# Cross attention in a decoder kernel: one product per head pair for values and key sums, and the division by query between two turns on TensorE

## What is computed

```python
q = (x @ Wq + bq).reshape(B, N, NUM_HEADS, HEAD_DIM)
k = (y @ Wk + bk).reshape(B, M, NUM_HEADS, HEAD_DIM)
v = (y @ Wv + bv).reshape(B, M, NUM_HEADS, HEAD_DIM)
scores = jnp.einsum('bnhd,bmhd->bhnm', q, k) * scale
attn = jax.nn.softmax(scores, axis=-1)
out = jnp.einsum('bhnm,bmhd->bnhd', attn, v).reshape(B, N, IMAGE_DIM)
h = jax.nn.relu(out @ W1 + b1)
return h @ W2 + b2
```

## Time and profile before

| | |
|---|---|
| Device time, three runs | 573.75, 574.8, 579.94 us; median 574.8 |
| Profiled execution, span from first to last instruction | 605.6 us |
| TensorE busy | 492.0 us (81%) |
| VectorE busy | 416.6 us (69%) |
| ScalarE busy | 297.0 us (49%) |
| POOL busy | 289.3 us (48%) |
| Granted TensorE clock, mean | 0.944 of full speed |

### The profile page before, as it was taken

The page is one execution under the profiler, slowest core; times in us unless marked ns, Lnnn a source line. Parts: engine busy times, 40 slices in busy tenths (PEclk is TensorE's granted clock), DMA queues, the critical chain, the costliest instruction groups (busy, mean ns, idle before and its releaser), DMA issues. The chain is left out here.

```text
span 605.6 us, 16577 instructions
## 1 busy us (share of the span) xinstructions
PE 492.0 (81%) x5675; PEld 367.1 (61%) x5675; DVE 416.6 (69%) x1308; ACT 297.0 (49%) x757; POOL 289.3 (48%) x540
## 2 busy tenths in 40 slices
PE   2979888888898888799999999998579887888820
PEld 1757666666666666467766766665357676676710
DVE  7568989998788878679989988875433323133337
ACT  2755556665655556246565655644153333223337
POOL 5454333333343331103577777768605665564630
PEclk9998999999999999689999999999699989797985
DMA  6643444555445553162333232311343323232149
GB/s 181 106 109 69 78 71 67 104 112 117 95 96 109 103 109 95 40 148 55 88 80 99 75 98 79 97 35 45 100 113 94 93 83 84 73 90 74 47 143 299
DMA packets 96002, 58.30 MB, mean 96 GB/s; under 512 B 24560, under 2 KB 92224, under 8 KB 95920
## 3 DMA queue, kind: packets, MB, share of 16 engines
q1 hardware_dynamic: 74448, 40.00, 28.6%
q10 hardware_dynamic: 16896, 7.34, 6.0%
q0 software_dynamic: 4576, 9.91, 5.0%
HBM read 20.83 MB, written 17.50 MB: 63 GB/s over the span
## 5 line engine op out<-in xcount | busy, mean ns | idle before, releaser
L758 DVE TENSOR_REDUCE nmax<-ps 128x8 f32<-128x512 f32 x128 | 85.5, 682 | 22.2 <-PE ps L1602 18.1
L507 POOL TENSOR_SCALAR veps<-mv 128x2 f32<-128x2 f32 x48 | 10.8, 225 | 162.2 <-issue 113.6
L1287 ACT ACTIVATE probs<-ps 128x512 f32<-128x512 f32 x128 | 73.5, 602 | 14.6 <-PE ps L1667 12.3
L602 POOL DMA_INDIRECT expert_in<-xn,sloti x64 | 65.4, 1022 | 17.9 <-issue 17.9
L1142 DVE TENSOR_TENSOR eh<-ps,sg 128x256 f32<-128x256 f32 x40 | 16.9, 424 | 75.7 <-ACT sg L1491 38.5
L655 POOL DMA_INDIRECT expert_out<-ey,xt x40 | 38.3, 957 | 38.6 <-DVE ey L1149 25.1
L2013 PE MATMUL ps<-wgu,turned 128*128 x160 | 44.0, 399 | 10.3 <-ACT turned L1485 9.0
L1485 ACT COPY turned<-ps 128x512 f32<-128x512 f32 (+1 forms) x43 | 23.9, 556 | 39.2 <-remote 16.2
L1602 PE MATMUL ps<-kbd,qs 96*64 96x128 bf16 x512 | 38.1, 293 | 5.8 <-DMA qs<-part 3.1
L1811 PE MATMUL ps<-x3T,shT 128*128 128x512 f32 x64 | 33.9, 659 | 6.5 <-DVE x_rows L968 2.5
L509 POOL TENSOR_TENSOR rstd<-veps,minus_half 128x2 f32<-128x2 f32 x48 | 36.8, 766 | 4.0
(11 more groups left out here) (247 smaller groups left out, 1359.0 us busy)
## 6 DMA issues: line engine op xcount, KB each, us to landing
kbd<-part SPq DMA_DIRECT2D x192, 32.0 KB
qs<-part ACTq DMA_DIRECT2D x93, 64.0 KB
xt<-expert_in SPq DMA_DIRECT2D x64, 72.0 KB
qs<-part SPq DMA_DIRECT2D x51, 64.0 KB
ck_scr<-wgu SPq DMA_DIRECT2D x6, 512.0 KB, 3.8
ckbd<-ck_scr SPq DMA_DIRECT2D x16, 192.0 KB, 2.9
kbd<-part SPq DMA_DIRECT2D x48, 64.0 KB
wgu<-in_L_ffn_gate_up_w SPq DMA_DIRECT2D x4, 512.0 KB, 3.9
```

Of the source, the lines that this page charges most:

```text
L602: pool.indirect_dma_start(xs, bass.IndirectOffsetOnAxis(sloti[b % 3][:, n:n + 1], 0), xn3[b % 3][:, n // TOPK, n % TOPK, :], None).then_in ...
L758: v.tensor_reduce(nmax[:, u, 8 * half:8 * half + 8], bank[:, :].rearrange("p (h k) -> p h k", k=64), AX.X, ALU.max, negate=True).then_inc( ...
L1287: a_.activation(probs[:, 2 * i:2 * i + 2, :], P2[i % 2][:, :].rearrange("p (j q) -> p j q", j=2), ACT.Exp, scale=SCALE).then_inc(s("probs" ...
```

## The change

`cvbd_all` gets the value columns of a pair in its first 16 columns and, in its last 16, ones for the keys of each head (eight columns per head). One product per pair then gives 16 rows of values and 16 rows of key sums, and the two pairs that share 32 partitions go to separate column halves of OD, so that the whole bank of 512 columns is filled. `cross_sums`, `cross_reciprocal` and `cross_spread` go, with their constants. ScalarE copies the whole bank to `att_raw`; TensorE turns it in four 128x128 transposes into MISC (`cross_turn`), where queries lie on the partitions; VectorE inverts one sum per head and query (128x32) and multiplies (128x256) into `rden`; TensorE turns that back in two transposes (`cross_turn_back`), and ScalarE copies it to `attT` (`cross_columns_of_heads`).

The order of calls changes: VectorE's `cross_body` does `stats`, `route_normalise`, `cross_attended` and then the row maxima; ScalarE's does `cross_raw` first, and the first exponentials ahead of the counts. The ones are written once, by a POOL copy in `lay_out_later_stages`; POOL's clear at the start covers only the first 16 columns. `route_twin`'s second copy counts on the same semaphore as its first, which takes one wait from `send`. Of the diff, the core (left out: unpacking of the constants, the size of `att_raw`, changed counts of the semaphore `set`):

```diff
--- before.py
+++ after.py
@@ -70,8 +70,6 @@
-    c["head_ones"] = (np.arange(46)[None, :] - 14 - (p // 64)[:, None]) % H == 0
-    c["head_spread"] = np.concatenate([p[:, None] == 32 * i + p[None, :] // D for i in range(4)], axis=1)
...
@@ -509,7 +505,7 @@
-            g.memset(cvbd_all[:, :, :, :], 0.0).then_inc(w_("zeroed"), 1)
+            g.memset(cvbd_all[:, :, :, 0:16], 0.0).then_inc(w_("zeroed"), 1)
@@ -558,6 +554,8 @@
+                g.tensor_copy(cvbd_all[:, :, :, 16:32].rearrange("p b j c -> p (b j) c"),
+                              key_ones[:, 0, 0:16].unsqueeze(1).to_broadcast([128, B * PAIRS, 16])).then_inc(w_("set"), 1)
             def self_body(b, p):
@@ -592,13 +590,13 @@
-            pool.wait_ge(w_("set"), 8)
+            pool.wait_ge(w_("set"), 9)
...
                 def send(b, n):
...
-                        wait_apart(pool, (r_("slot"), b + 1), (r_("named"), b + 1), (r_("twin"), b + 1))
+                        wait_apart(pool, (r_("slot"), b + 1), (r_("twin"), 2 * b + 2))
@@ -967,15 +965,16 @@
-                def cross_reciprocal(b):
-                    dve.wait_ge(c_("od"), 2 * b + 2)
-                    v.reciprocal(rden[:, 0:64], MISC[:, 0:64]).then_inc(c_("rden"), 1)
                 def cross_attended(b):
-                    dve.wait_ge(c_("rden_ps"), b + 1)
-                    at_least(dve, c_("h_ps"), b)
-                    dve.wait_ge(c_("att_raw"), b + 1)
-                    v.tensor_tensor(attT[:, :], att_raw[:, :], ATT_SPREAD, ALU.mult).then_inc(c_("attT"), 1)
+                    dve.wait_ge(c_("od_turned"), b + 1)
+                    cells = MISC[:, :].rearrange("p (t m r) -> p t m r", t=2, r=32)
+                    v.reciprocal(rsum[:, :, :, :], cells[:, :, :, 16::D]).then_inc(c_("shares"), 1)
+                    dve.wait_ge(c_("shares"), 2 * b + 1)
+                    at_least(dve, c_("attT_ps"), b)
+                    v.tensor_tensor(rden[:, :].rearrange("p (m t a d) -> p t m a d", t=2, a=2, d=D),
+                                    cells[:, :, :, 0:16].rearrange("p t m (a d) -> p t m a d", a=2),
+                                    rsum[:, :, :, :].unsqueeze(4).to_broadcast([128, 2, S // 32, 2, D]), ALU.mult).then_inc(c_("shares"), 1)
                 def cross_end(b):
...
@@ -1015,18 +1014,15 @@
                 def cross_body(b):
-                    if has(b - 1):
-                        cross_reciprocal(b - 1)
...
+                    if routed(b - 2):
+                        route_normalise(b - 2)
+                    if has(b - 1):
+                        cross_attended(b - 1)
...
-                    if routed(b - 2):
-                        route_normalise(b - 2)
-                    if has(b + 1):
...
-                    if has(b - 1):
-                        cross_attended(b - 1)
@@ -1071,7 +1067,6 @@
                 def last_bodies():
...
-                    cross_reciprocal(B - 1)
@@ -1393,7 +1388,7 @@
-                            row_of[:, bass.ds(4 * b, 4)].unsqueeze(2)).then_inc(r_("named"), 1)
+                            row_of[:, bass.ds(4 * b, 4)].unsqueeze(2)).then_inc(r_("twin"), 1)
                 def route_logits(b):
@@ -1412,24 +1407,31 @@
                 def cross_raw(b):
...
-                    at_least(act, c_("attT"), b)
-                    a_.copy(att_raw[:, :], OD[:, 0:S]).then_inc(c_("att_raw"), 1)
+                    at_least(act, c_("od_turned"), b)
+                    a_.copy(att_raw[:, :], OD[:, :]).then_inc(c_("att_raw"), 1)
+                def cross_columns_of_heads(b):
+                    act.wait_ge(c_("attT_ps"), b + 1)
+                    act.wait_ge(*((c_("h_ps"), b) if b else (s_("wo_ps"), B)))
+                    a_.copy(attT[:, :], MISC[:, 0:S]).then_inc(c_("attT"), 1)
                 def cross_body(b):
...
+                    if has(b - 1):
+                        cross_raw(b - 1)
...
+                    if has(b) and b > 0:
+                        exps(c_, b, (0,))
...
-                    if has(b - 1):
-                        cross_raw(b - 1)
-                    if has(b) and b > 0:
-                        exps(c_, b, (0,))
...
+                    if has(b - 1):
+                        cross_columns_of_heads(b - 1)
@@ -1445,6 +1447,7 @@
                 def last_bodies():
...
+                    cross_columns_of_heads(B - 1)
@@ -1831,27 +1834,25 @@
-                        mm(OD[rows:rows + 32, 0:S], cvbd_all[:, b, j, :], probs[:, at, :],
-                           start=(j % 2 == 0), stop=(j % 2 == 1), skip_group_check=True)
-                def cross_sums(b, half):
-                    if half == 0:
-                        if b == 0:
-                            pe.wait_ge(s_("gtmp"), B)
-                        at_least(pe, c_("h"), 2 * b)
-                        at_least(pe, c_("attT"), b)
-                    for at, j in steps_of(half):
-                        for c in range(4):
-                            last = mm(MISC[32 * c:32 * c + 32, 0:64], head_ones[:, 14 - 2 * j:46 - 2 * j], probs[:, at, 64 * c:64 * c + 64],
-                                      start=(at == 0), stop=(at == PAIRS - 1), skip_group_check=True)
+                        last = mm(OD[rows:rows + 32, S * (j % 2):S * (j % 2) + S], cvbd_all[:, b, j, :], probs[:, at, :],
+                                  start=(j % 2 == 0), stop=True, skip_group_check=True)
...
-                def cross_spread(b):
-                    pe.wait_ge(c_("rden"), b + 1)
-                    for c in range(4):
-                        last = mm(ATT_SPREAD[:, 64 * c:64 * c + 64], head_spread[:, 128 * c:128 * c + 128], rden[:, 0:64],
-                                  start=True, stop=True)
-                    last.then_inc(c_("rden_ps"), 1)
+                def cross_turn(b):
+                    pe.wait_ge(c_("att_raw"), b + 1)
+                    at_least(pe, c_("h"), 2 * b)
+                    if b == 0:
+                        pe.wait_ge(s_("gtmp"), B)
+                    for i in range(4):
+                        last = tr(MISC[:, i * 128:(i + 1) * 128], att_raw[:, i * 128:(i + 1) * 128], ident[:, :])
+                    last.then_inc(c_("od_turned"), 1)
+                def cross_turn_back(b):
+                    pe.wait_ge(c_("shares"), 2 * b + 2)
+                    for u in range(2):
+                        last = tr(MISC[:, u * 128:(u + 1) * 128], rden[:, u * 128:(u + 1) * 128], ident[:, :])
+                    last.then_inc(c_("attT_ps"), 1)
                 def cross_hidden(b):
@@ -1902,6 +1903,8 @@
+                    if has(b - 1):
+                        cross_turn(b - 1)
@@ -1910,7 +1913,7 @@
-                        cross_spread(b - 1)
+                        cross_turn_back(b - 1)
@@ -1926,7 +1929,6 @@
-                        cross_sums(b, 0)
@@ -1934,11 +1936,11 @@
-                        cross_sums(b, 1)
                 def last_bodies():
...
-                    cross_spread(B - 1)
+                    cross_turn(B - 1)
+                    cross_turn_back(B - 1)
...
@@ -2045,7 +2047,7 @@
-            cell = jj * 48 + a * D
+            cell = jj * 32 + a * D
...
```

More of the change, by code:

```diff
@@ L129, in decoder @@
         shift_pair = held["shift_pair"][SHIFT:128].rearrange("p (j a) -> p j a", a=2).unsqueeze(3)
-        head_ones, head_spread = held["head_ones"], held["head_spread"]
         key_ones = held["key_ones"].rearrange("p (j c) -> p j c", j=2)
@@ L186, in decoder @@
         ckbd = [sb(f"ckbd{i}", [128, PAIRS, 2, M], BF16) for i in range(2)]
-        att_raw = sb("att_raw", [128, S])
+        att_raw = sb("att_raw", [128, 2 * S])
         b2_part = [sb(f"b2_part{i}", [128, E], BF16) for i in range(3)]
@@ L244, in decoder @@
         P1, P2, OD = PS[2:4], PS[4:6], PS[6]
-        ATT_SPREAD = MISC[:, 256:256 + S]
         TT, GU, YT = PS[0:2], PS[2:4], (PS[4], PS[7])
@@ L991, in route_normalise @@
                     if b == 0:
-                        dve.wait_ge(w_("set"), 8)
+                        dve.wait_ge(w_("set"), 9)
                     for u in range(2):
@@ L1957, in last_bodies @@
                     shared_out(0, OD)
-                pe.wait_ge(w_("set"), 5)
+                pe.wait_ge(w_("set"), 6)
                 for b in range(B):
```

## The result

| | |
|---|---|
| Kernel before, beside it | 574.95 us, median |
| Changed kernel, four runs | 582.12 to 592.21 us, median 586.52 |
| Ratio | 1.0163, 95% interval 1.0117 to 1.0209 |
| The same kernel once more, four runs | 582.46 to 591.08, median 588.75; ratio 1.0198 (1.0128 to 1.0268) |
| Predicted | 577.6, range 569 to 587 |

The ratio leaves out the run of 592.21 us, which is more than 1.5% above the fastest of its kernel. The first median is in the range, close to its upper end; the second, 588.75, lies above it. The forecast itself, no measurable change, is not what happened: the kernel became 1.6 to 2.0% slower.

The account below looks back on a forecast made before the run. A closed POOL and VectorE loop of 10.26 us was taken to bound the cross stage. Early bodies +1.8, steady +0.5, body 14 +1.2, last body +0.3, start -1.0 make +2.8 on 574.8: 577.6 us, range 569 to 587.

Parts of the forecast that it names:

- What bounds the kernel before: Steady cross-attention bodies: POOL (4.9 us) and VectorE (5.35 us) alternate in a closed loop of 10.26 us, TensorE beside it.
- Rival A: Cross stage: TensorE was the bound after all, so 1.3 us less per body and about 561 us; chance 0.13.
- B: Rival, cross stage: the reordered chain is longer than summed, giving 584 or 585 us; chance 0.25.
- C: Rival, cross stage: TensorE's clock falls to half in three or four episodes, giving about 588 us; chance 0.12.
- The prices of the parts: New cross-stage instructions: reciprocal 0.40 us, product 0.41, 512-wide copy 0.56, copy to attT 0.4.
- None of the POOL loop is shortened: Steady cross bodies: POOL's loop stays; one wait fewer before the first send gives at most 0.05 us per body.
- This is the part that costs: VectorE's reorder in cross_body: row maxima come last, making a new loop of 10.3 us; ten steady bodies add +0.5 us.
- The early bodies: Cross intervals 1-2, 2-3 and 3-4, formerly below 10.3 us, lengthen by +0.7, +0.8 and +0.3: +1.8 us.
- Body 14 and the drain: End of the cross stage: the longer chain shows whole in body 14, +1.2 us, and +0.3 in the last body.
- The start: Kernel start: constants shrink by 286 KB, so the start gains 0 to 1.35 us, taken as -1.0.
- POOL's new fill: Self body 0: the 128x2048 fill falls where POOL idles 1.68 us; at most 9.4 us, counted as nothing.
- 78% against those 64%: Argument against a clock fall: the new body keeps TensorE busy 8 of 10.3 us, the earlier half-clock stretch 2.56 of 4.

Follow-up runs that it names:

- before_rstd_first: Kernel before, with POOL's second rstd moved ahead of the first two sends; 570.71 us, ratio 0.9937.
- rest_later: Changed kernel with VectorE's cross_rest one call later, behind the row maximum of scores (1,0); 581.86 us, ratio 1.0128.
- fill: Changed kernel plus eight unread bf16 products per body on TensorE in front of the turn back; 579.71 us, ratio 1.0101.
- after_again: Changed kernel measured and profiled once more, unchanged; 588.75 us, ratio 1.0198.
- rstd_first_fill: Changed kernel with POOL's second rstd ahead of the first two sends and unread products, eight or more per body, before the turn back; 577.6 us, ratio 1.0042.
- rstd_first: Changed kernel with POOL's second rstd moved ahead of the first two sends; 583.55 us, ratio 1.0139.

## Why the prediction was right or wrong

**What bounds the kernel before: right.** POOL and VectorE alternate, TensorE stands beside them. before_rstd_first shows it by taking POOL's sends out of the loop. Rival A falls with it: TensorE's work shrank and the bodies did not.

**The range: right in part by luck.** The sum was +2.8 us, and the two medians lie 11.6 and 13.1 us above those of the kernel before beside them. That 586.5 is inside 587 is owed to the room that the range left for B and for C's low end, and the larger part of the loss is C's.

**The prices of the parts: right.** Reciprocal 0.35 us (0.40 taken), product 0.42 (0.41), the 512-wide copy 0.59 (0.56), the copy to `attT` 0.37 (0.4).

**"None of the POOL loop is shortened", and it was taken as unchanged: a term of the sum that was mis-sized.** The loop became 0.16 us longer per body, not 0.05: the second `veps` takes 0.34 us against 0.24 and the first send 1.15 against 1.08. The first part is shown by rest_later: in the new order `cross_rest`, with two inputs in SBUF, runs while POOL makes `veps`. The Trainium skill ("SBUF — State Buffer", Who interferes with whom) says that a VectorE instruction with two SBUF inputs contends with a GpSimd instruction that reads SBUF; the trace agrees, by 0.1 us here. That the first send is longer for a like reason (VectorE's `route_normalise` now runs beside it) was not tried.

**"This is the part that costs", of the reorder: wrong.** The chain that it makes was summed well: 10.3 us by the sum, 10.21 measured once POOL's loop is out of the way. That it runs through the logits, as the sum has it, is not shown: VectorE's own 9.24 us of work and its waits fill those bodies as well. But the comparison was with the wrong thing. With the new arithmetic the old order gives 11.02 us at full clock, where reciprocal, product and turn back stand behind both row maxima and TensorE waits 2.40 us for them instead of 1.23; the reorder repairs most of that. The early bodies, at full clock (run fill): 1-2 takes 9.14 where +0.7 on about 9.5 was expected; 2-3 takes 10.16 against 9.47 (+0.7, +0.8 expected); 3-4 takes 10.73 against 10.08 (+0.65, +0.3 expected). That bodies 1 to 13 come to +2.4 us at full clock, where the sum has +2.3, is luck: the early ones give +1.0 instead of +1.8, the others +1.4 instead of +0.5.

**Body 14 and the drain: +1.5 us forecast, +2.5 at full clock by the table.** The mechanism is not tested by a run of its own. There the pipeline has no more work to lay over the added hand-overs, and copy, turn, reciprocal, product, turn back and copy stand one behind the other.

**The start: right at the start, unclear behind it.** The first matmul came at 7.94 us against 8.84, near the -1.0 of the forecast; before, then after:

```profile
8.84 0.69 PE L1571 MATMUL ps<-constants,xn 128*128 128x128 f32 x2 [8.84 <-DMA wv<-in_L_attn_Wv]
```

```profile
7.94 0.47 PE L1574 MATMUL ps<-constants,xn 128*128 128x128 f32 x1 [7.94 <-DMA wv<-in_L_attn_Wv]
```

POOL's new fill of 2048 columns took 1.90 us (run after_again, L557), about the 1.68 us that POOL had idled there, so to count nothing for it was right within 0.2 us. At body 0 of the cross stage 0.4 us is left of the earlier start in these two profiles. Kernels with the same start reach that body between 258.25 and 262.3 us, so a single profile can't say whether the gain stays.

**Rival C was put aside too cheaply: the step that failed.** The forecast counted nothing for the clock and gave its fall 12%, at a price of 588 us. It fell, and the median is 586.5 to 588.8. The argument against it was "78% against those 64%": a busy share of one body beside one of another stage. TensorE was in fact busy 109.9 of 140 us, 78%, and its clock fell all the same. But the body's own wait of 1.2 us in front of the turn back had been foreseen, together with 1.3 us of matmuls less; each was entered as harmless, since it hung on no chain. Run fill shows what most of the fall cost: 7 to 9 us, got back by work that nobody reads. By the marks it is 3.0 us in bodies 1 to 13, 2.8 in the next and about 4 in the drain, 9.8 of the 14.4 us, the last two read from rstd_first_fill. In the kernel before, TensorE was busy 132.4 of those 140 us at full clock; that the removed products were what held it there is inferred, as rest_later held it without them up to 404 us.

**Open.** What decides in which body the clock falls: the changed kernel fell at 284 to 292 us in both profiles, rest_later and rstd_first, with the same wait, did not in theirs. And which edits would bring the changed arithmetic to the 9.7 us that the old one reaches: three chains (POOL's sends, what stands behind the routing `rstd`, the scores to the row maxima) stand within 0.4 us of one another in it, and each attempt uncovered the next.

## What to carry to other kernels

Work taken off an engine that is not the bound gains nothing by itself, and on TensorE it can lose: look at the granted clock after, and at where the new idle time stands. Before a serial hand-over is made cheaper, look at whose loop sets the spacing; here two calls exchanged on POOL in the old kernel brought 0.6%, and the whole rewrite cost 1.6 to 2.0%. Where several chains are within a few per cent of one another, price each by the run that removes the others.

## What the runs showed of the hardware

- Eight bf16 products of 128x256 (1.04 us) per body, read by nobody, made the kernel 7 to 9 us faster in the median: in the profile the granted clock stayed at 1.00 from 264 to 396 us where it had fallen to 0.62 in two stretches of 4 us.
- With a wait of 2.40 us in each body of 11.0 to 12.6 us the mean clock of 140 us was 0.90; with that wait filled to 0.43 us, in bodies of 11.0 us, it was 1.00.
- A wait of 1.23 us per body went with falls in one kernel and with none in another of nearly the same busy time (109.9 and 110.7 us of 140).
- VectorE's 128x256 subtraction of two SBUF tiles lengthened a POOL instruction that ran beside it from 0.25 to 0.34 us.
